# Four unfolded square products and an earlier order of loads in a layernorm, decay attention and mixture-of-experts kernel

## What is computed

```python
qkv = layernorm(x) @ w_qkv                      # 512 x 1536
q, k = elu(q) + 1, elu(k) + 1                   # 16 heads of 32
running_kv   = decay_scan(k * v, sigmoid(decay), 0)   # s_t = decay * s_{t-1} + x_t
running_ksum = decay_scan(k,     sigmoid(decay), 0)
den = clip(sum(q * running_ksum), 1e-6)
x = x + (q * running_kv / den) @ w_out
h = layernorm(x)
comb = top-2 of softmax(h @ gate_w)             # 8 experts
routed = sum_e comb_e * (silu(h @ w_gate[e]) * (h @ w_up[e])) @ w_down[e]   # inner width 352
shared = (silu(h @ sw_gate) * (h @ sw_up)) @ sw_down                          # inner width 704
x = x + routed + shared
```

## Time and profile before

| | |
|---|---|
| three runs | 677.13, 683.62, 686.48 us |
| median | 683.62 us |
| the profiled execution's own time | 681.28 us |
| its span, first to last instruction | 679.5 us |
| PE busy | 646.2 us (95%) |
| DVE, ACT, POOL busy | 416.2, 267.8, 222.7 us |
| mean granted clock of the tensor engine | 0.989 |

### The profile page before, as it was taken

The page is one execution under the profiler, slowest core; times in us unless marked ns, Lnnn a source line. Parts: engine busy times, 40 slices in busy tenths (PEclk is TensorE's granted clock), DMA queues, the critical chain, the costliest instruction groups (busy, mean ns, idle before and its releaser), DMA issues.

```text
span 679.5 us, 11781 instructions
## 1 busy us (share of the span) xinstructions
PE 646.2 (95%) x3787; PEld 426.7 (63%) x3788; DVE 416.2 (61%) x754; ACT 267.8 (39%) x407; POOL 222.7 (33%) x266
## 2 busy tenths in 40 slices
PE   7989999999999999999998999999999999999991
PEld 7766777767677656666655656666666666666550
DVE  7786987997998755767778776533333333333330
ACT  5363462464453445465665765311111111111110
POOL 6320131231103227222332241244444444434421
PEclk9998999999999999999999999999999999999997
DMA  6840012513425697586684424388777877889852
GB/s 233 309 133 16 15 48 66 167 47 94 125 63 175 185 248 191 160 187 170 162 188 137 72 42 87 65 148 137 133 127 134 137 131 137 133 134 126 136 76 40
DMA packets 110388, 86.89 MB, mean 128 GB/s; under 512 B 79280, under 2 KB 85424, under 8 KB 110352
## 3 DMA queue, kind: packets, MB, share of 16 engines
q1 hardware_dynamic: 88848, 43.94, 27.9%
q0 software_dynamic: 12864, 29.50, 25.5%
q10 hardware_dynamic: 8640, 12.98, 5.8%
HBM read 44.45 MB, written 23.33 MB: 100 GB/s over the span
## 4 chain that ended last, share of the span: by engine, by line
PE 55%; DMA 10%; DVE 7%; issue 3%; ACT 1%; POOL 1%; SPq 1%; POOLq 0%; DVEq 0%; ACTq 0%
PE ps_y L535 15%; PE ps_u L535 14%; PE ps_g L535 14%; PE ring L393 8%; DMA out_dram<-y_job,job_tok 5%; PE turn_h L555 3%; DMA x_in<-x_job 2%; DMA x_job<-xn_scratch,job_tok 2%; DVE routed L1484 1%; DMA xn_scratch<-xn_hl 1%; DMA out_dram<-x 1%; DVE hid L1427 1%; DVE col_max L1463 1%; DVE den L1359 0%; PE ps_norm L410 0%
## 5 line engine op out<-in xcount | busy, mean ns | idle before, releaser
L1145 ACT CAST hidT<-turn_h 128x384 f16<-128x384 f32 x71 | 33.9, 478 | 173.1 <-PE turn_h L555 168.2
L989 POOL DMA_INDIRECT out_dram<-y_job,job_tok x39 | 61.8, 1585 | 98.9 <-DVE y_job L1769 60.0
L393 PE MATMUL ring<-xnT_h,wq_h 128*128 128x512 f32 x192 | 79.4, 413 | 4.2 <-DVE xnT_l L1298 2.0
L535 PE MATMUL ps_y<-routed,hidT 128*128 x351 | 82.1, 379 | 1.3 <-DVE hidT L1420 1.3
L535 PE MATMUL ps_g<-routed,x_in 128*128 x468 | 82.6, 313 | 0.5 <-DMA x_in<-x_job 0.5
L393 PE MATMUL ring<-xnT_h,wq_l 128*128 128x512 f32 x192 | 77.3, 403 | 0.0
L393 PE MATMUL ring<-xnT_l,wq_h 128*128 128x512 f32 x192 | 77.1, 402 | 0.0
L535 PE MATMUL ps_u<-routed,x_in 128*128 x468 | 76.2, 312 | 0.0
L1427 DVE SCALAR_TENSOR_TENSOR hid<-ps_u,job_hid,silu 128x352 f32<-128x352 f32 x39 | 22.8, 584 | 85.5 <-PE ps_u L535 83.3
L535 PE MATMUL ps_y<-shared,hidT 128*128 128x512 f16 x288 | 67.4, 379 | 3.7 <-DVE hidT L1420 3.7
L896 POOL TENSOR_SCALAR var_eps<-mean_var 128x1 f32<-128x1 f32 x32 | 12.3, 384 | 171.9 <-DVE mean_var L1406 93.4
(11 more groups left out here) (246 smaller groups left out, 1095.5 us busy)
## 6 DMA issues: line engine op xcount, KB each, us to landing
x_res<-in_L_attn_x_dram SPq DMA_DIRECT2D x18, 256.0 KB, 3.6
routed<-in_L_ffn_w_gate_dram ACTq DMA_DIRECT2D x6, 704.0 KB, 4.7
routed<-in_L_ffn_w_up_dram ACTq DMA_DIRECT2D x6, 704.0 KB, 6.5
out_dram<-x SPq DMA_DIRECT2D x16, 256.0 KB, 3.5
xn_scratch<-xn_hl SPq DMA_DIRECT2D x16, 256.0 KB, 2.6
out_dram<-y_job POOLq DMA_DIRECT2D x16, 256.0 KB
x_in<-in_L_attn_x_dram SPq DMA_DIRECT2D x14, 256.0 KB, 2.7
routed<-in_L_ffn_w_down_dram ACTq DMA_DIRECT2D x6, 512.0 KB, 7.2
```

The source lines that it names most:

```text
L393: ins = pe.matmul(ps, a, b, start=(i == 0), stop=(i == len(steps) - 1))
L535: ins = pe.matmul(ps, a[i][:, k, :], w(j, k), start=(start and q == 0), stop=(stop and q == len(steps) - 1))
L989: pool.indirect_dma_start(out[:, :], bass.IndirectOffsetOnAxis(job_tok[:, r:r + 1], 0), y_job[:, b, :], None, compute_op=ALU.add).then_inc ...
L1145: act.copy(hidT[:, 0], turn_h[:, 0:FC, :]).then_inc(s["hidTh_s"], 1)
```

## The change

1. Routed gate and up squares: no fold on POOL. `column_norms` waits for the squares themselves and multiplies all four quarters of 352 columns by ones (four products instead of two). DVE still folds the shared matrices' squares.
2. Part 11 of the projection lands in `last_raw` instead of a slot of `w_raw`, so it is loaded without a wait; the four parts of the output matrix move one slot on. The first half of the shared down matrices' loads waits for all twelve parts.
3. x tiles 4 to 7 are loaded right after part 12 and ahead of the shared matrices; tiles 6 and 7 land in `x_res` (until now 6 and 7 followed in `x_in` after the shared matrices). The residual rows 0 and 1, which also use `x_res`, are loaded later, once eight tiles have been normalized, behind x tiles 8 and 9.
4. The decay parameters (four DMAs of single values) are issued by ACT as its first instructions, no longer by POOL between its two `lo_w` and its constants.
5. In DVE's order `lo_w` of parts 2 and 3 moves behind `lo_x` of tiles 2 and 3. The very first K product waits only for the rounded halves of its parts; it does the eight matmuls with `wq_h` first and then the four with `wq_l`, each with a wait for its own part.
6. In DVE's order `lo_x` of the second next tile moves ahead of `lo_gate` and `max_step`, at c = 2 of each block.

```diff
+        turn_of = lambda m: m - FREE_PARTS - (m >= QKV_PARTS)
+        def raw(m):
+            if m < FREE_PARTS:
+                return num[:, m // KC, m % KC, :]
+            if m == QKV_PARTS - 1:
+                return last_raw[:, 0:D]
+            return w_raw[:, (turn_of(m) % 3) * D:(turn_of(m) % 3 + 1) * D]
...
         def x_rows(t):
-            return (x_res if t in (2, 3) else x_in)[:, t % 2, :]
+            return (x_res if t in (2, 3, 6, 7) else x_in)[:, t % 2, :]
...
             def column_norms(m):
-                w = pieces[m][3]
-                pe.wait_ge(s["fold_s"], m + 1)
+                x, kind, h, w = pieces[m][0:4]
+                if x < E and kind < 2:
+                    pe.wait_ge(s["square_s"], m + 1)
+                else:
+                    pe.wait_ge(s["fold_s"], m + 1 if x == E else SHARED_PIECES + x + 1)
...
                 n = w.shape[1] // 4
-                for k in range(2):
+                parts = 4 if x < E else 2
+                for k in range(parts):
                     ins = pe.matmul(norms_of(m), ones_h[:, :], squares[:, k * n:(k + 1) * n],
-                                    start=(k == 0), stop=(k == 1))
+                                    start=(k == 0), stop=(k == parts - 1))
...
-                if n == 0 and c == 0:
-                    pe.wait_ge(s["w_lo"], KC * {1: 1, 2: 2, 0: 3}[z] - EARLY_W)
-                    pe.wait_ge(s["w_lo_e"], EARLY_W)
+                first = n == 0 and c == 0 and z == 1
+                if first:
+                    pe.wait_ge(s["w_hi"], KC)
+                elif n == 0 and c == 0:
+                    pe.wait_ge(s["w_lo"], KC * {2: 2, 0: 3}[z] - EARLY_W)
...
+                for k, ((wh, wl), (xh, xl)) in enumerate(pairs):
+                    pe.matmul(ps[:, :], wh, xh, start=(k == 0), stop=False)
+                    pe.matmul(ps[:, :], wh, xl, start=False, stop=False)
+                for k, ((wh, wl), (xh, xl)) in enumerate(pairs):
+                    if k < EARLY_W:
+                        pe.wait_ge(s["w_lo_e"], k + 1)
+                    else:
+                        pe.wait_ge(s["w_lo"], k + 1 - EARLY_W)
+                    ins = pe.matmul(ps[:, :], wl, xh, start=False, stop=(k == KC - 1))
...
             def load_x(t):
                 if t >= TPB:
-                    sp.wait_ge(s["xn1"], t - 1)
+                    sp.wait_ge(s["xn1"], t - 3 if t < 2 * TPB + 2 else t - 1)
...
             def load_part(m):
-                if m >= FREE_PARTS + 3:
-                    sp.wait_ge(s["w_lo"], m - 2 - EARLY_W)
+                if m >= QKV_PARTS:
+                    sp.wait_ge(s["w_lo"], m - 3 - EARLY_W if turn_of(m) < 6 else m - 2 - EARLY_W)
...
             for m in range(4, QKV_PARTS + 1):
                 load_part(m)
-            load_res(0)
-            load_res(1)
-            load_x(TPB)
-            load_x(TPB + 1)
+            for t in range(TPB, 2 * TPB):
+                load_x(t)
...
             sp.wait_ge(s["over_0"], 1)
+            sp.wait_ge(s["w_lo"], QKV_PARTS - EARLY_W)
...
+                if n == 0:
+                    load_x(2 * TPB)
+                    load_x(2 * TPB + 1)
+                    load_res(0)
+                    load_res(1)
...
-            for g in range(P // DH):
-                pool.dma_start(dec[g * DH:(g + 1) * DH, :], ...)
...
-                        fold(norm_unit(u))
...
+            for g in range(P // DH):
+                act.dma_start(dec[g * DH:(g + 1) * DH, :], ...)
             for t in range(TPB):
                 hi_x(t)
                 hi_w(t)
...
             lo_x(1)
-            lo_w(EARLY_W)
             lo_x(2)
-            lo_w(EARLY_W + 1)
             lo_x(3)
-            for m in range(TPB, QKV_PARTS):
+            for m in range(EARLY_W, QKV_PARTS):
                 lo_w(m)
...
                 query(n, 2)
+                next_x(lo_x, 1)
                 if n == 0:
                     lo_gate()
                 max_step(n * KC + 2)
-                next_x(lo_x, 1)
```

More of the change, by code:

```diff
@@ L245, in preln_decay_attention_moe @@
         pm.close()
-        names = """wk0 wk1 wk2 wk3 wk4 wk5 wk6 wk7 w_in0 w_in1 w_in2 w_hi w_lo w_lo_e ones_s consts dec_in dec_e dec_1 dec_ok gw_in
+        names = """wk0 wk1 wk2 wk3 wk4 wk5 wk6 wk7 w_in0 w_in1 w_in2 w_last w_hi w_lo w_lo_e ones_s consts dec_in dec_e dec_1 dec_ok gw_in
             xl0 xl1 xs0 xs1 stat1 var1 veps1 rstd1 shift1 xn1 turned1 hi1 lo1 k_mm v_mm q_mm k_act q_act
@@ L306, in preln_decay_attention_moe, with raw_in @@
         FREE_PARTS = 2 * KC
[L307 to L310, removed]
+        turn_of = lambda m: m - FREE_PARTS - (m >= QKV_PARTS)
[5 more added lines that the diff above has]
+            return w_raw[:, (turn_of(m) % 3) * D:(turn_of(m) % 3 + 1) * D]
+        def raw_in(m):
+            if m < FREE_PARTS:
+                return s[f"wk{m}"], 16
+            if m == QKV_PARTS - 1:
+                return s["w_last"], 16
+            return s[f"w_in{turn_of(m) % 3}"], 16 * (turn_of(m) // 3 + 1)
         part_cols = lambda m: slice((1, 2, 0)[m // KC] * D, ((1, 2, 0)[m // KC] + 1) * D)
@@ L322, in x_rows @@
         def x_rows(t):
-            return (x_res if t in (2, 3) else x_in)[:, t % 2, :]
+            return (x_res if t in (2, 3, 6, 7) else x_in)[:, t % 2, :]
         def x_loaded(t):
-            return (s[f"xs{t % 2}"], 16) if t in (2, 3) else (s[f"xl{t % 2}"], 16 * (t // 2 + (t < 2)))
+            if t in (2, 3, 6, 7):
+                return s[f"xs{t % 2}"], 16 * (1 + t // 6)
+            return s[f"xl{t % 2}"], 16 * (1 if t < 2 else 2 if t < 6 else t // 2 - 1)
         def turned_x(t):
@@ L396, in column_norms @@
             def column_norms(m):
-                w = pieces[m][3]
-                pe.wait_ge(s["fold_s"], m + 1)
+                x, kind, h, w = pieces[m][0:4]
[3 more added lines that the diff above has]
+                    pe.wait_ge(s["fold_s"], m + 1 if x == E else SHARED_PIECES + x + 1)
                 if m:
                     pe.wait_ge(s["max_s"], m)
-                x, kind, h = pieces[m][0:3]
                 if kind == 2:
@@ L447, in project @@
                     pairs.append(((wq_h[:, k, cols], wq_l[:, k, cols]), (xnT_h[:, n % 2, k, :], xnT_l[:, n % 2, k, :])))
-                split_product(ps[:, :], pairs).then_inc(s[name + "_mm"], 1)
+                if not first:
+                    split_product(ps[:, :], pairs).then_inc(s[name + "_mm"], 1)
+                    return
+                for k, ((wh, wl), (xh, xl)) in enumerate(pairs):
[7 more added lines that the diff above has]
+                    ins = pe.matmul(ps[:, :], wl, xh, start=False, stop=(k == KC - 1))
+                ins.then_inc(s[name + "_mm"], 1)
             def sum_heads(n, c):
@@ L754, in load_res @@
                 else:
-                    sp.wait_ge(s["xn1"], TPB)
+                    sp.wait_ge(s["xn1"], 2 * TPB)
                 sp.dma_start(x_res[:, t % 2, :], xf[t * P:(t + 1) * P, :]).then_inc(s[f"xr{t % 2}"], 16)
@@ L829, in _ @@
                 for j in (0, 1):
-                    if n and n + 1 < NB:
+                    if 1 < n and n + 1 < NB:
                         load_x((n + 1) * TPB + j)
@@ L835, in _ @@
                     store_tile((n - 2) * TPB + 3)
-                if n + 1 < NB:
+                if 0 < n and n + 1 < NB:
                     load_x((n + 1) * TPB + 2)
@@ L920, in _ @@
                 lo_w(m)
-            for g in range(P // DH):
-                pool.dma_start(dec[g * DH:(g + 1) * DH, :], bass.AP(decay.tensor, g, [[0, DH], [P // DH, KC]]),
-                               allow_slow_non_contiguous=True).then_inc(s["dec_in"], 16)
             const(pool.memset(head_of[:, :], 1.0))
@@ L990, in scatter @@
                                         y_job[:, b, :], None, compute_op=ALU.add).then_inc(s[f"yo{b}"], 16)
[L992 to L997, removed]
             const(pool.memset(zeros[:, :], 0.0))
@@ L1007, in _ @@
             for t in range(NT - AHEAD + 1):
-                for u in (2 * t, 2 * t + 1):
-                    if norm_unit(u) is not None and pieces[norm_unit(u)][1] < 2:
-                        fold(norm_unit(u))
                 add_shared(t)
@@ L1018, in _ @@
                 gather(r)
[L1019 to L1022, removed]
                 if r < AHEAD - 1:
@@ L1121, in upper @@
                     .then_inc(s["upper_s"], 1)
+            for g in range(P // DH):
+                act.dma_start(dec[g * DH:(g + 1) * DH, :], bass.AP(decay.tensor, g, [[0, DH], [P // DH, KC]]),
+                              allow_slow_non_contiguous=True).then_inc(s["dec_in"], 16)
             for t in range(TPB):
```

## The result

The changed kernel takes 675.78 us (median; fastest 674.35), the kernel before, run beside it, 682.75 us. The ratio is 0.992, with a 95% interval of 0.9896 to 0.9945: 5.5 us less, between 3.8 and 7.1. The medians are 7.0 apart; the ratio leaves out the runs that are over 1.5% above the fastest of their kernel. The forecast was 676.3 us, 7.3 less than before. The direction holds, the gain is three quarters of the forecast one, and one of the terms, the price of edit 4, was wrong.

A forecast was written before the change was run, and what follows sets the result against it. PE, busy 95%, was taken to bound the kernel. Block 0 -7.8, block 1 -0.3 and norm products +0.8 sum to -7.3 us: 676.3 us from the median of 683.62, range 669 to 684.

The forecast's parts named there:

- Start, edits 2 and 5: Start of block 0: K starts at 13.2 us without a gap, V waits 1.3, Q starts at 20.1, 3.4 us gained.
- Edit 4: Start: decay loads issued by ACT cost nothing, 0.5 us as the far end; POOL gets 2.5 us free.
- Rest of block 0, edits 3 and 6: Block 0: tile 6 wait and clock fall go; block 1 starts at 52.4, -7.8 us including the start; 0.3 more later.
- Norm products, edit 1: Shared stage: added products cost +4.8 us, `hidT` waits shrink by 2.96, the late fold gives -1.0; sum +0.8 us.
- Sum: Whole kernel: -7.8 - 0.3 + 0.8 = -7.3 us, 676.3 us on the median of 683.62; chance 0.46.
- A: Start: clock falls in the new 1.3 us gap before V, +1.5 us; total -5.8, 677.8 us; chance 0.18.
- B: Shared stage: `hidT` waits come from DVE's own chain, shrink only 1.2; total -5.5, 678.1 us; chance 0.10.
- C: Start: part 11 lands no earlier, Q starts at 23.4 as before; total -3.9, 679.7 us; chance 0.09.
- D: Routed stage: pace set by its DMA round; at 6.10 us it costs 9.8, total +2.5, 686.1 us; chance 0.07.
- E: Block 0: DVE waits less than counted, -9.0, and the `lo_x` move gives 0.6; total -8.8, 674.8 us; chance 0.10.

The follow-up runs named there:

- e1: Changed kernel with the decay loads issued by SP behind projection part 11 and ahead of part 12: 672.95 us, ratio 0.9882 to the kernel before.
- e12: e1 with part 11 waiting on SP until the rest of part 8 is written, decay loads ahead of that wait: 677.01 us, ratio 0.9924.
- e5: e1 with the first V and Q products also waiting only for rounded halves and taking their rests last: 672.36 us, ratio 0.9867.
- e4: Changed kernel with POOL's fold, two norm products and the wait for the fold back in: 678.52 us, ratio 0.9938.
- e2: Changed kernel with the decay loads back on POOL between its `lo_w` and its constants: 673.57 us, ratio 0.9888.
- e7: Kernel before with only the decay loads moved, issued by ACT as its first instructions: 685.41 us beside 682.63, ratio 1.0041.
- e10: e1 with DVE writing the rest of x tile 5 after its other four steps again: 675.95 us, ratio 0.993.
- e11: e1 plus one load of 128 pieces of 64 bytes into scratch as ACT's first instruction: 675.56 us, one run.
- e6: e1 with x tiles 6 and 7 loaded behind the shared matrices: 678.94 us, ratio 0.9952.
- e3: Changed kernel with the second half of the routed gate and up squares left out of the norms, two products: 671.74 us, ratio 0.9845.
- e8: Changed kernel with the four decay loads issued twice by ACT, the second four into scratch: 677.45 us, one run.
- e9: e1 with part 11, and the decay loads behind it, waiting on SP until the rest of part 8 is written: 681.31 us, ratio 1.0004.

## Why the prediction was right

**Start, edits 2 and 5: right.** In e1, where the first tile is on time, K starts at 13.21 (13.2 predicted) and V at 17.56 (17.3). Edit 2 by itself is worth 2.4 us (e12). The gap before V that edit 5 leaves is there, 1.28 us for 1.3, and what it costs is open (e5).

**Edit 4, the failed step.** I put it at nothing, with 0.5 us as the far end, from 128 packets on POOL's queue and from ACT's idle time. ACT's time was indeed free (the four issues took 1.87 us). The price lies in the loads: the first tile's statistics are 1.15 us late, part 0 reaches ACT at 10.88 instead of 7.82, and the clock fell behind the longer gap before the first turn. Together that is 2.4 us at K and 2.5 at block 1 (55.81 against 53.3). e4 has the loads without the fall: 1.6 at K and 1.5 at block 1 (54.78), so about 1.0 of the 2.5 is the fall. Not doing it gives 0.9882 and 0.9888 (e1, e2) instead of 0.992, and doing it alone 1.0041 (e7). The earlier trace rows was the wrong row: it showed these values through another queue, at another time, when no first load was in flight. Through ACT's queue they are 576 packets, not 128. In eight profiled executions without a load on ACT's queue at the start the statistics began at 3.31 to 3.72, in six with one at 4.62 to 4.99. The late second tile is no sure sign of these loads: it is at 5.90 to 6.11 in those six, at 4.28 to 4.54 in seven of the eight, but at 5.86 in e10, without such a load.

The Trainium skill (DMA: Bandwidth & Descriptors, Issuing engines are not separate DMA queues) says that loads of all issuers run on the same 16 DMA engines and interleave. The direction that the prediction drew from it came out, the first tile 1.15 us later; I gave it no price. The reason isn't settled. Shared room on the engines doesn't account for it: the extra packets fill 2.3% of them (0.7% in e11), and from 6 to 8 us, where the kernel before has them 0.91 busy, they are only 0.40 busy. Two effects have to be told apart. At the first tile the number of loads made no difference (4.69 with four, 4.62 with eight, 4.99 with one of another shape), so there the runs point to a second queue's being at work at all. For the loads behind it the number does count. SP's queue moved 3.17 to 3.55 MB in the first 12 us of the eight executions without a load from ACT, 3.06 with one, 2.01 to 2.03 in the four with four, and 1.69 with eight.

**Rest of block 0, edits 3 and 6: right.** The wait for tile 6 and the second fall of the clock are gone. With e1's start, block 1 begins at 53.3, 0.9 later than replayed: 0.3 us at V, 0.2 more at `query(2)`, the rest at V(3) and `run_kv` (49.76 against 48.8). Edit 3 is worth 2.5 us (e6), edit 6 1.6 (e10). With edit 2's 2.4 that is 6.5 of the 6.9 that e1 gains up to block 1; edit 5 wasn't undone by itself. These sizes are read at block 1, one execution each. By the ratios e6 lies 4.8 us above e1, e10 3.3 and e12 2.9, but e1's interval alone is 3 us to either side, so the times don't settle them.

**Norm products, edit 1: right in mechanism, +0.4 for +0.8.** From first shared to first routed gate product it took 214.9 us before and 215.3 after. The added products cost 4.1 us where the prediction has 4.8 (e3). The four waits for `hidT` fell from 3.0 to 0.3 us, the late fold's 1.69 is gone, and DVE's scale step is at 0.163 us where it averaged 0.527 with the fold (e4). With the fold back the stage takes 0.3 more. Edit 1 is neither gain nor loss that these runs can tell.

**Sum.** Up to the first shared product edits 2 to 6 gave 4.5 us instead of 8.1, then edit 1 took 0.4 instead of 0.8. At the first routed product the profile has -4.1, and the ratio's -5.5 (-3.8 to -7.1) holds that, while my -7.3 lies just outside. That the median came out within 0.5 us of the forecast is partly luck: 676.3 was counted from a median of 683.62, and 5.5 off that is 678.1.

**The rivals.** A is wrong: the clock stayed up behind gaps of 1.27 to 1.41 us before V in every execution looked at (the changed kernel, e1, e3, e6, e10, e12). B is wrong: `hidT` comes in time without the folds. C is wrong: ACT takes part 11 at 19.67 in the changed kernel without waiting. D, the routed stage at the pace of its loads, shows in small: 2.3 us of waits for `x_in` in the profiled execution, none in e1's, 3.9 in e4's, 4.7 in e7's, 0.5 before. It differs from execution to execution and may account for a part of the spread of times; that wasn't tried by itself. E wasn't reached.

The best version of the whole change is e1 (e2 and e5 are the same within what can be measured): 672.95 us, 1.2% under the kernel before. Its interval and the changed kernel's overlap; but e1's fastest run is 672.11 and e2's 672.3, where the fastest of 19 runs of the changed kernel is 674.35, and the profiles show where the 2.5 us lie. e3, at 671.74, is no version to use: it leaves half of the squares out of the norms.

## What to carry to other kernels

A load at the very start is priced by what it does to the first link of the chain and to the loads behind it, not by its bytes and not by a row of the same load on another queue at another time; put it behind the first tiles, where its reader's slack covers it. Replay the handovers engine by engine, and when a gap is closed on one engine, name the one that is late next. Before a landmark of two executions is compared, see whether both started alike: e5's block 1 looked as if the closed gap gave nothing, but its start was 1.3 us late. Added products on the engine that bounds the kernel can be paid for by waits that they remove. Here 4.1 us of products took the place of a POOL step that held DVE up, and the sign was in the trace of before: the two steps ended within 0.02 us of each other.

## What was not expected of the hardware

One load of 128 pieces of 64 bytes issued by ACT while SP issued its first loads put the first statistics from 3.54 to 4.99 us (one run); four loads of single values put them at 4.67 to 4.70, and eight at 4.62. And with 576 packets of single values, 2 KB in all, SP's queue moved 1.15 MB less in the first 12 us (2.02 MB in e7, 3.17 in the kernel before, with the same order of SP's loads), while the DMA engines were less busy (from 6 to 8 us 0.43 for 0.91).

The clock's falls don't follow from a gap's length alone. Before the first turn, it fell after gaps of 2.10, 2.15, 2.24 and 2.33 us (changed kernel, e3, e10, e7) and not after 1.89 or 1.96 (e8, e4). Before K, it fell after 1.97 and 2.38 (e8) and not after 1.60 (e7). Before Q, it fell after 2.06 (e9) and not after 2.27 (e12) or 1.94 (e7). At the turn of tile 6, it fell after 3.04, 3.93 (e7) and 1.91 (e9), and stayed at 1.00 behind 3.28 (e6) and 2.38 (e10). So a gap of some 2 us can cost a fall or nothing; a fall cost about 1 us at the start (e4 against the changed kernel) and by the prediction's count 1.5 elsewhere. That is probably a part of what separates executions of one kernel.

In e11 and e5, behind gaps of 2.13 and 0.86 us before the first turn, the rows give a granted clock of 1.00, and yet the turn took 1.09 us instead of 0.63 and the 14 small products behind it 1.70 instead of 0.94. So at the start the pace has to be read from the products, not from the clock's column alone.
